# Flamingo gated block: the first steps of the attention pipeline reordered, shorter fills, the first context in pieces

## What is computed

```python
x = x + tanh(g_xattn[0]) * xattn(layernorm(x), ctx_1024, Wq, bq, Wk, bk, Wv, bv, Wo, bo)
x = x + tanh(g_ffn[0]) * ffn(layernorm(x), router_w, expert_bias, w_gate, w_down, w_gate_shared, w_down_shared)

def xattn(x, context, ...):            # 16 heads of depth 8
    q = x @ Wq.T + bq
    k = context @ Wk.T + bk
    v = context @ Wv.T + bv
    attn = softmax(einsum('bhtd,bhcd->bhtc', q, k) / sqrt(8))
    return einsum('bhtc,bhcd->bhtd', attn, v).reshape(B, T, D) @ Wo.T + bo

def ffn(x, ...):                       # 160 experts, the 8 largest sigmoid weights are used
    routed = einsum('eti,ehi->th', silu(einsum('th,eih->eti', x, w_gate)) * combine.T[:, :, None], w_down)
    return routed + silu(x @ w_gate_shared.T) @ w_down_shared.T
```

## Time and profile before

| | before |
|---|---|
| time, median of 3 runs | 1283.6 us (1283.05 to 1288.66) |
| span of the profiled execution | 1272.8 us |
| around the span, against the median | 10.8 us |
| PE busy | 1198.3 us (94%) |
| DVE busy | 1041.6 us (82%) |
| ACT busy | 925.3 us (73%) |
| POOL busy | 287.0 us (23%) |
| steps 0 to 3 end at (L1127, or the first L1025 of the next step) | 50.15, 69.55, 103.60, 127.32 us |

### The profile page before, as it was taken

One profiled execution on the slowest core, in us unless ns is written; L12 is line 12 of the kernel. 1 busy time (PEld: TensorE's weight loads), 2 busy tenths in 40 slices (PEclk: granted clock), 3 DMA queues, 4 the chain that ended last, 5 costly groups with the idle time before them and its releaser, 6 DMA issues.

```text
span 1272.8 us, 39247 instructions
## 1 busy us (share of the span) xinstructions
PE 1198.3 (94%) x12826; PEld 798.5 (63%) x12826; DVE 1041.6 (82%) x1855; ACT 925.3 (73%) x1998; POOL 287.0 (23%) x418
## 2 busy tenths in 40 slices
PE   2669999999999999999999999887999999999998
PEld 1337777777777777777777777665455554444444
DVE  6757787787787787778878878864899999999998
ACT  2437777776776777776777777665788888888887
POOL 7153423422422432342243242100000000000000
PEclk9879999999999999999999999988999999999999
DMA  4243343343333334334334333204699999999996
GB/s 127 60 137 90 107 112 105 102 113 110 99 106 112 100 103 113 92 111 115 98 102 119 104 102 98 57 19 114 161 224 225 227 225 228 227 226 227 227 226 149
DMA packets 64776, 171.80 MB, mean 135 GB/s; under 512 B 16264, under 2 KB 32712, under 8 KB 64744
## 3 DMA queue, kind: packets, MB, share of 16 engines
q1 hardware_dynamic: 55784, 150.39, 49.1%
q0 software_dynamic: 8960, 20.99, 5.2%
HBM read 120.41 MB, written 12.55 MB: 104 GB/s over the span
## 4 chain that ended last, share of the span: by engine, by line
PE 89%; DVE 5%; DMA 3%; ACT 2%; issue 1%; SPq 1%; DVEq 0%; ACTq 0%
PE bank L996 16%; PE bank L1225 14%; PE bank L1025 14%; PE bank L1198 13%; PE bank L1010 13%; PE bank L1072 5%; PE bank L1058 5%; PE bank L1051 3%; PE bank L1087 1%; PE bank L1106 1%; PE bank L1115 1%; DMA ctx_in<-in_ctx_dram 1%; DMA v_sb<-c_scratch 1%; PE bank L1100 1%; SPq L332 1%
## 5 line engine op out<-in xcount | busy, mean ns | idle before, releaser
L537 ACT ACTIVATE p_exp<-bank 125x448 f32<-125x448 f32 x768 | 401.2, 546 | 222.3 <-PE bank L1010 221.9
L756 DVE TENSOR_REDUCE part_max<-bank 128x1 f32<-128x500 f32 x672 | 440.9, 673 | 76.0 <-PE bank L1025 73.0
L1010 PE MATMUL bank<-q_st,k_stk 97*125 97x224 f16 x1536 | 275.3, 265 | 4.6 <-ACT p_exp L537 4.6
L1025 PE MATMUL bank<-kparts,q_blk 128*128 128x500 f16 x672 | 258.2, 386 | 11.0 <-DVE part_max L756 8.9
L1225 PE MATMUL bank<-ctT,w_ring 128*128 128x448 f16 x960 | 234.5, 353 | 3.1 <-DVE ctT L911 3.1
L1010 PEld LDWEIGHTS bank<-q_st,k_stk 97*125 97x125 f16 x1536 | 194.3, 139 | 66.0 <-ACT p_exp L537 21.4
L996 PE MATMUL bank<-p_exp,v_sb 125*32 125x168 f32 (+1 forms) x6144 | 229.6, 268 | 0.6 <-ACT p_exp L537 0.6
L651 ACT ACTIVATE ctT<-bank 128x448 f32<-128x448 f32 x320 | 173.7, 543 | 42.5 <-PE bank L1198 24.3
L996 PEld LDWEIGHTS bank<-p_exp,v_sb 125*32 125x32 f32 x6144 | 162.2, 110 | 67.5 <-ACT p_exp L537 1.6
L911 DVE TENSOR_TENSOR ctT<-k_stk,ctT 128x448 f16<-128x448 f32 x320 | 197.7, 618 | 0.3 <-ACT ctT L657 0.2
L657 ACT ACTIVATE ctT<-k_stk 128x448 f16<-128x448 f32 x320 | 182.1, 569 | 3.6 <-DVE k_stk L905 3.5
(11 more groups left out here) (142 smaller groups left out, 1354.7 us busy)
## 6 DMA issues: line engine op xcount, KB each, us to landing
v_sb<-c_scratch SPq DMA_DIRECT2D x114, 448.0 KB, 9.1
k_stk<-kparts SPq DMA_DIRECT2D x384, 93.8 KB, 2.2
ctx_in<-in_ctx_dram SPq DMA_DIRECT2D x32, 750.0 KB
k_stk<-c_scratch SPq DMA_DIRECT2D x38, 448.0 KB, 9.2
w_scratch<-w_out POOLq DMA_DIRECT2D x80, 128.0 KB, 2.0
w_ring<-w_scratch SPq DMA_DIRECT2D x80, 128.0 KB, 7.7
w_in<-in_L_ffn_w_gate_dram POOLq DMA_DIRECT2D x80, 64.0 KB, 2.2
w_in<-in_L_ffn_w_down_dram POOLq DMA_DIRECT2D x80, 64.0 KB, 2.3
```

The source lines that it names most:

```text
L537: act.activation(p_exp[0:KP, j % PR, f * 448:(f + 1) * 448], ST[f][0:KP, 0:448], ACT.Exp).then_inc(exp_done, 1)
L756: v.reduce_max(part_max[:, i // NCH, i % NCH:i % NCH + 1], SM[(back(step, 1)[1] + i) % 2][:, 0:CK], axis=AX.X).then_inc(sm_maxed, 1)
L1010: last = pe.matmul(ST[f][0:KP, (g % 2) * GC:(g % 2 + 1) * GC], k_stk[0:97, u, g, j * KP:(j + 1) * KP], q_st[0:97, u, g, :, :].rearrange("p ...
L1025: pe.matmul(SM[(u + i) % 2][:, 0:CK], rows, kparts[:, u, 0, c * CK:(c + 1) * CK], start=True, stop=True).then_inc(sm_done, 1)
```

## The change

It reorders the set-up and the first steps, and narrows the value product. In the order of the diff: the value product uses 25 columns (`VW`) of each value tile; a new stage `rows_here` at step 3, slot 11 waits for the output weights. The context of batch 0 comes in three transfers with a semaphore each, the first ahead of the biases. The small inputs move behind the first query rows, the output weights ahead of step 2. The rest of the query rows is stacked in three parts, in SP's steps 1, 2 and 3, between the key rows and the negated maxima. SP asks for the next context at the start of each step. On POOL the first weight loads move behind the masks; the fills of `v_sb` (only the columns of ones) and of one row of `k_stk` (1500 elements) move ahead of step 0; two DMAs of SP copy that row to the seven others. POOL waits for the first query rows inside step 1 and for the rest ahead of step 4, and adds the constant ahead of step 3. DVE clears OB once.

```diff
+    VW = 3 * d + 1
-    CONSTANT_AT, BANK_FREE_AT = (1, 11), (2, 1)
+    CONSTANT_AT, BANK_FREE_AT, ROWS_AT = (1, 11), (2, 1), (3, 11)
...
-        IDENT, MASKS, V_ONES, K_ONES = 2, 11, 12, 13
+        IDENT, MASKS, K_ONES, V_ONES = 2, 11, 12, 14
-        QROWS = 2 * 16 * 3 * HG
+        QROWS = 16 * 3 * HG
+        REST_ROWS_AT = {1: (0,), 2: (1,), 3: (2,)}
...
+            if 4 in before:
+                before[4]()
             with eng.Fori(2, loop_to // 2) as h:
...
+            def load_chunk(c):
+                j = slice(c * TPC, (c + 1) * TPC)
+                sp.dma_start(ctx_in[:, 0, j, :], ctx[0].rearrange("(p j) c -> p j c", j=KT)[:, j, :])\
+                  .then_inc(first_here[c], 16)
...
+            load_chunk(0)
             for dst, src in ((bqc, bq), (bkc, bk), (bvc, bv)):
                 sp.dma_start(dst[:, :], src.rearrange("(p a) -> p a", a=1)).then_inc(bias_in, 16)
-            sp.dma_start(ctx_in[:, 0, :, :], ctx[0].rearrange("(p j) c -> p j c", j=KT)).then_inc(ctx_here[0], 16)
+            for c in range(1, NCH):
+                load_chunk(c)
             load_x(*REST, x_rest)
...
-                for g in range(HG):
-                    for r, part in enumerate((q_hi, q_lo, q_hi)):
+                for r in parts:
+                    part = (q_hi, q_lo, q_hi)[r]
+                    for g in range(HG):
...
-            stack_queries(0, 1)
...
-            stack_queries(1, NTC)
+            stack_queries(0, 1, (0, 1, 2), q_rows)
+            small_inputs()
+
+            def ones_rows():
+                sp.wait_ge(consts, K_ONES)
+                for u, g0 in ((0, 1), (1, 0)):
+                    sp.dma_start(k_stk[96:97, u, g0:HG, :],
+                                 k_stk[96:97, 0, 0:1, :].to_broadcast([1, HG - g0, C])).then_inc(k_ones, 16)
...
+            ones_rows()
...
             def body(step):
+                load_ctx(step)
                 if on(step, 1):
...
-                if on(step, -1) and not (isinstance(step[0], int) and num(step) < 1):
-                    ...
+                if isinstance(step[0], int) and num(step) in REST_ROWS_AT:
+                    stack_queries(1, NTC, REST_ROWS_AT[num(step)], q_rest_rows)
...
-            attention(sp, body, B - 2)
+            attention(sp, body, B - 2, {2: output_rows})
...
-            load_pair((0, 0))
             const(pool.memset(head_mask[:, :], 1.0))
...
+            load_pair((0, 0))
+            const(pool.memset(k_stk[96:97, 0, 0, :], 1.0))
+            assert made[0] == K_ONES
+            const(pool.memset(v_sb[:, :, :, 0:4, 3 * d:VW], 1.0))
+            const(pool.memset(v_sb[:, :, :, 4:VG, d:VW], 1.0))
...
-            def ones():
-                const(pool.memset(v_sb[:, :, :, :, :], 1.0))
-                assert made[0] == V_ONES
-                const(pool.memset(k_stk[96:97, :, :, :], 1.0))
-                assert made[0] == K_ONES
+            def first_rows():
+                pool.wait_ge(q_rows, QROWS)
+
+            def all_rows():
                 pool.wait_ge(q_hi_done, NTC)
-                pool.wait_ge(q_rows, QROWS)
+                pool.wait_ge(q_rest_rows, QROWS)
...
+                if isinstance(step[0], int) and num(step) == 1:
+                    first_rows()
...
-            attention(pool, body, B - 2, {1: ones, 2: add_constant})
+            attention(pool, body, B - 2, {3: add_constant, 4: all_rows})
...
-                v.tensor_tensor(sd[:, 1, :], SH[0:I, I:I + D], sd[:, 0, :], ALU.subtract).then_inc(sh_lo, 1)
+                link(v.tensor_tensor(sd[:, 1, :], SH[0:I, I:I + D], sd[:, 0, :], ALU.subtract))
+                v.memset(OB[:, 0:OC], 0.0).then_inc(ob_cleared, 1)
...
-                    last = pe.matmul(OB[32 * (g % 4):32 * (g % 4) + 32, at:at + w],
-                                     v_sb[0:KP, u, j, g, :], p_exp[0:KP, j % PR, src:src + w],
+                    last = pe.matmul(OB[32 * (g % 4):32 * (g % 4) + VW, at:at + w],
+                                     v_sb[0:KP, u, j, g, 0:VW], p_exp[0:KP, j % PR, src:src + w],
...
-                            if c == 0:
-                                pe.wait_ge(ctx_here[u], h * 16 + 16)
+                            if isinstance(h, int) and b == 0:
+                                pe.wait_ge(first_here[c], 16)
+                            elif c == 0:
+                                pe.wait_ge(ctx_here[u], h * 16 + (16 if u else 0))
```

More of the change, by code:

```diff
@@ L208, in flamingo_gated_block @@
         ctx_here = [sem(f"ctx_here{i}") for i in range(2)]
+        first_here = [sem(f"first_here{i}") for i in range(NCH)]
         kst_here = [sem(f"kst_here{i}") for i in range(2)]
@@ L288, in _, with small_inputs, stack_queries @@
                 sp.dma_start(w_raw[:, n, :], w).then_inc(weights_in, 16)
+            load_chunk(0)
             for dst, src in ((bqc, bq), (bkc, bk), (bvc, bv)):
                 sp.dma_start(dst[:, :], src.rearrange("(p a) -> p a", a=1)).then_inc(bias_in, 16)
-            sp.dma_start(ctx_in[:, 0, :, :], ctx[0].rearrange("(p j) c -> p j c", j=KT)).then_inc(ctx_here[0], 16)
+            for c in range(1, NCH):
+                load_chunk(c)
             load_x(*REST, x_rest)
[L293 to L296, removed]
             sp.dma_start(ctx_in[:, 1, :, :], ctx[1].rearrange("(p j) c -> p j c", j=KT)).then_inc(ctx_here[1], 16)
[L298 to L301, removed]
+            def small_inputs():
+                sp.dma_start(bo_b[:, :], row(bo).to_broadcast([PT, D])).then_inc(small_in, 16)
+                sp.dma_start(eb_b[:, :], row(expert_bias).to_broadcast([PT, E])).then_inc(small_in, 16)
+                for n, g in enumerate((g_xattn, g_ffn)):
+                    sp.dma_start(g_raw[:, n:n + 1], row(g).to_broadcast([PT, 1])).then_inc(small_in, 16)
+                sp.dma_start(sh_raw[0:I, 0, :], w_gate_shared).then_inc(late_in, 16)
+                sp.dma_start(sh_raw[:, 1, 0:I], w_down_shared).then_inc(late_in, 16)
+                sp.dma_start(r_raw[:, :, :], router_w.rearrange("(a p) h -> p a h", a=2)).then_inc(late_in, 16)
+            def stack_queries(c0, c1, parts, here):
                 sp.wait_ge(q_hi_done, c1)
@@ L305, in stack_queries, with output_rows, load_ctx @@
                 cols = slice(c0 * TC, c1 * TC)
-                for g in range(HG):
-                    for r, part in enumerate((q_hi, q_lo, q_hi)):
+                for r in parts:
+                    part = (q_hi, q_lo, q_hi)[r]
+                    for g in range(HG):
                         sp.dma_start(q_stk[32 * r:32 * r + 32, g, cols], part[32 * g:32 * g + 32, cols])\
-                          .then_inc(q_rows, 16)
-            stack_queries(0, 1)
[L313 to L318, removed]
-            stack_queries(1, NTC)
+                          .then_inc(here, 16)
+            stack_queries(0, 1, (0, 1, 2), q_rows)
[5 more added lines that the diff above has]
+                                 k_stk[96:97, 0, 0:1, :].to_broadcast([1, HG - g0, C])).then_inc(k_ones, 16)
+            def output_rows():
+                sp.wait_ge(wp_cp, 4)
+                sp.wait_ge(o_cleared, 1)
+                for h in range(H):
+                    g, c = (h // 3, h % 3) if h < 12 else (h - 12, 3)
+                    p0 = 32 * g + (d * c if c < 3 else 0)
+                    sp.dma_start(wo_m[p0:p0 + d, c, :], woT[d * h:d * h + d, :]).then_inc(wo_rows, 16)
+            ones_rows()
+            def load_ctx(step):
+                if on(step, -1) and not (isinstance(step[0], int) and num(step) < 1):
+                    h, u = back(step, -1)
+                    b = num((h, u))
+                    sp.wait_ge(t_done, (b - 1) * NCH)
+                    sp.dma_start(ctx_in[:, u, :, :], ctx[bass.ds(b, 1)].rearrange("a (p j) c -> p (a j) c", j=KT))\
+                      .then_inc(ctx_here[u], 16)
             def body(step):
+                load_ctx(step)
                 if on(step, 1):
@@ L789, in tokens @@
                 if c == 0:
[L790 removed]
+                    dve.wait_ge(q_rest_rows, QROWS)
                 dve.wait_ge(xh_cp, c + 1)
@@ L977, in bank_free, with rows_here @@
             def bank_free():
-                pe.wait_ge(consts, K_ONES)
+                pe.wait_ge(k_ones, 32)
+                pe.wait_ge(consts, V_ONES)
                 pe.wait_ge(sh_cp, 3)
-                pe.wait_ge(sh_lo, 2)
+                pe.wait_ge(sh_lo, 1)
                 pe.wait_ge(constant_made, 1)
+                pe.wait_ge(ob_cleared, 1)
+            def rows_here():
                 pe.wait_ge(wo_rows, 16 * H)
@@ L1128, in body @@
                     aside(step, k, (TOKENS_REST_AT, lambda: query_tokens(2, 1, NTC)),
-                          (Q_REST_AT, lambda: queries(1, NTC)), (BANK_FREE_AT, bank_free),
+                          (Q_REST_AT, lambda: queries(1, NTC)), (BANK_FREE_AT, bank_free), (ROWS_AT, rows_here),
                           *((at, lambda c=c: tokens(c)) for at, c in TOKENS_AT.items()),
```

11 lines of the change are left out of this document (3 added, 8 removed).

## The result

The changed kernel takes 1265.47 us (median of 4 runs, 1258.74 to 1268.03); the kernel before, run beside it, 1283.32 us (4 runs, 1280.14 to 1288.66). The ratio is 0.9846, 95% interval 0.9815 to 0.9877: 17.9 us faster. Forecast was 22.0 us less, 1261.6 us, range 1255.5 to 1270.0.

What follows compares the result with a forecast made beforehand. TensorE sets the pace from 103.60 us on; before that, waits bound the start. Sum: 5.25 + 3.2 + 10.1 + 1.9 + 2.2 - 0.4 - 0.3 = 22.0 us off the 1283.6 median, 1261.6 us, range 1255.5 to 1270.

Steps and rivals of the forecast that it cites:

- Second memset: Set-up: the long `k_stk` fill holds VectorE's 12-column `stat` in the layer norm; filling less gains 5.25 us.
- First memset: Set-up: `bv_rep`, held by GpSimd's DMA issuing and memset, is let go at 19.1 in place of 22.7; gain 3.6 us.
- Rival A: The held `bv_rep` goes free at once, near 15.6, another 2.9 us earlier: 1258.7 us; chance 0.2.
- Pieces: First context in three pieces: worth nothing by itself, and delays the biases, costing some 0.4 us.
- SyncE's order: Earlier context request removes TensorE's 10.1 us wait in step 2; SP's queue makes step 3 late by 0.3 us.
- rival C: SP's queue is late in step 3, for the context or rows behind it: +4, 1265.6 us; chance 0.13.
- Clock in step 2: Without the wait, step 2 runs at the upper clock level, some 22 us in place of 23.9: gain 1.9 us.
- Narrow loads: Value product loads 25 of 32 columns; one exposed load in each of 384 groups saves 5.8 ns: 2.2 us.
- rival E: Value product with 25 rows loses the four-strip overlap: 1861 us; chance 0.01.
- D: Value group is bound by its loads, so narrowing gains 33 us more: 1228 us; chance 0.03.
- Additions: DVE's added memset of one bank with a link loses 0.4 us; moved `add_constant` and earlier context requests cost nothing.
- Rival B: Context transfer delays the key rows in every loop step; 1305 us at 1.5 us a step; chance 0.05.

Runs made afterwards that it cites:

- light loop: Kernel before and changed kernel, each with half of the expert loop's weight broadcast left out; medians 1270.68 us and 1253.41 us.
- early_bv: Changed kernel with only `bv_rep` moved ahead of the first query chunk on VectorE; 1265.16 us (one run).
- both_more: Changed kernel with output weights stacked one step earlier and `bv_rep` ahead of the first query chunk; 1262.49 us (6 runs), ratio to before 0.9854.
- one_piece: Changed kernel with the first context in one transfer behind the biases; 1269.01 us (one run).
- ctx_late: Changed kernel with each step's context load issued behind that step's key rows in SyncE's queue; 1283.0 us (one run).
- wide_32: Changed kernel with all 32 columns in the value product in place of 25; 1272.61 us (one run).
- after_again: Changed kernel once more, unchanged, second profile; 1265.22 us (4 runs), ratio 0.9864.
- after_third: Changed kernel a third time, unchanged; 1263.51 us (6 runs), ratio 0.9875.

## Why the prediction was right, and where it was not

The forecast of 1261.6 us stands 3.9 us below the 1265.47 measured; 17.9 us gained of the 22.0 predicted. Over the four profiles of this change (one with the light loop) the last marker comes at 817.07, 819.10, 819.35 and 819.10, mean 818.7; over the three of the kernel before (one with the light loop), at 839.14, 837.75 and 835.37, mean 837.4. That is 18.8 us, in line with the medians. The first pair's 22.07, just the number forecast, was partly luck.

By the means of these profiles the gain is 9.4 us in step 0, 1.2 in step 1, 9.0 in step 2, -3.4 in step 3 and 2.6 in the rest. The sum had 8.45 (its parts 1 to 3), nothing, 11.6 (parts 4 and 5, less the additions), -0.3 and 2.2. The mechanisms are the right ones; the total is near because misses of both signs partly cancel.

1. *Second memset, 5.25 us:* right. `stat` takes 0.17 us. The fills took 1.34, 0.26 and 1.54 us, 0.3 more than forecast, and VectorE's work near 8 us was not held.
2. *First memset, release at 19.1:* the step failed by which the instruction that follows the DMAs holds the write until it ends. `bv_rep` ended at 17.32, 17.15 and 17.26 in the three profiles, some 0.3 us into GpSimd's last weight issue, and the first key product began at 17.97, for 22.79 before. Rival A was wrong too; the truth lies between, 1.8 us from the forecast. The Trainium skill, SBUF — State Buffer, section Who interferes with whom, has whoever issues first keep the pair. The trace agrees where a memset was running before VectorE's operation (`early_bv`: asked at 10.18 while the memset of 10.12 ran, ended at 11.73, as that ended); it does not agree for the operation that was there before the memset, which stood 7.4 us in each profile of the kernel before. `both_more` shows it again: `bv_rep` stood from 10.05, when a first memset was running until 10.07, and ended at 11.74, with the next one, which began at 10.13.
3. *Pieces, cost 0.4 us and no gain:* the cost is right (`xnT` 0.33 us later), the gain was left out. That "DVE's held write, not the context, releases the next product" held only as long as `bv_rep` stood until 19.1; `one_piece` shows 1.4 us at the end of step 0, and none at the last marker. Parts 1 to 3 together: step 0 ends 9.2 us earlier in the first pair, 8.45 by the sum.
4. *SyncE's order, 10.1 less 0.3 us:* the mechanism is right, shown from the other side by `ctx_late`. Two sizes were off. The wait that goes is not 10.1 us but 10.1, 7.2 and 5.2 in three profiles of the kernel before, 7.5 in the mean: one execution was taken for the kernel. And step 3 loses more than 0.3: against 23.67 us it took 24.22, 26.54, 28.61 and 29.29, so 0.5 to 5.6 us, 3.5 in the mean. The step that failed is the sum of 12.4 us to the request and 10.5 for the transfer: it followed the context only, and not the twelve key rows, the query rows and the negative row queued behind it, whose issue took SyncE until 85 us. That is rival C, which had 0.13; it took place with the other gains, not in place of them.
5. *Clock in step 2, 1.9 us:* step 2 took 23.70 us in the first profile (clock 0.93) and 22.13 in the three others, the 22 forecast. But in just those three step 3 waits longer. Counted from the start of step 2, TensorE arrives 1.6 us earlier, and the negative row is issued no earlier: at 25.5 us in the first profile and at 26.1 to 27.3 in the others. So steps 2 and 3 together take 47.9 us in the first, and 48.7, 50.7 and 51.4 in the others. Nothing of the clock's gain is left behind step 3.
6. *Narrow loads, 2.2 us:* 1.7 measured, by both the changed kernel and `wide_32`. 0.11 us in a pair of steps, over its 24 groups, is 4.6 ns a group (an estimate, on a difference of 0.01 us steps): one exposed load in each was the right count. The mean duration of a load fell by 6 ns, 110 to 104, near the 5.8 in proportion to the columns; the busy time over the number of loads, which the sum started from, fell by 1.5, since it counts overlapping loads once. The Trainium skill, TensorEngine Tiling (Array Packing), section Restrictions, asks that the active columns not exceed the limit of the column tiling; the trace agrees, with 25 of 32 columns in a strip: rival E did not happen, nor D.
7. *Additions, 0.4 us:* the memset took 0.24 us, and with its link it puts VectorE's next `part_max` off by 0.35 us (0.55 us behind the start of the operation before it, 0.20 before the change); nothing else was seen. Rival B did not happen: the pair of loop steps has no wait.

The step "10.8 us lie around the span" was wrong as well: it is 1.5. It did no harm, because 22.0 was taken off the median.

## What to carry to other kernels

An engine's queue is late for its last entry, not its first: when a block of transfers is moved ahead of others, add up the issue time down to the row that is wanted soonest. A profiled execution may lie at the low end of its kernel's runs; compare stages against a fixed marker, and a stage full of transfers against its rate, before the ends of two spans are subtracted. A small operation that stands for microseconds points at the engine beside it, and filling less there is a cheap cure, but what it gives up may be taken by the next cause, here the context and the queue.

## What the runs showed of the hardware

- In an otherwise equal instruction order, `bv_rep` stood 7.4 us (15.32 to 22.71, a long memset behind the weight issues) and 0.87 us (15.15 to 16.02, short memsets there). Nothing that GpSimd did up to 17.2 differs but for the size of what follows. No run here explains it.
- A stage of the same instructions, with DMA share 1.04, ran at 215 to 226 GB/s in twelve profiles, and from the last marker to the end it took 433.7 to 454.7 us; with half of the broadcast left out the spread of the runs was 6.0 and 3.0 us.
- Two executions of one kernel, alike up to 40.9 us, differ in the stretch that follows: at the low clock from 42.4 to 49.3 us or at the high one throughout, and step 1 took 20.34 or 17.65 us (`after_again`, `after_third`). No run here explains it.
